# Two-batch top-3 mixture on one core: second weights issued together, bias products in pairs, product tiles stored in one transfer

## The reference, cut to what matters

```python
x_addr = x_flat @ P_w.T
dw1 = _route_dense(x_addr @ U1.T, 3, 1.0)    # 3 of 12 experts for each token, softmax weights
dw2 = _route_dense(x_addr @ U2.T, 3, 1.0)
dw3 = _route_dense(x_addr @ U3.T, 3, 1.0)
h = _apply_mixture(x_flat, dw1, W1)          # W1: 12 x 1024 x 256
h = gelu(h)
y = _apply_mixture(h, dw2, W2)               # W2: 12 x 256 x 1024
y = y + dw3 @ b2                             # b2: 12 x 256
```

## Time and profile before

| what | value |
|---|---|
| median of 3 runs | 1136.07 us (1131.33 to 1138.95) |
| the profiled execution's own time | 1138.42 us |
| its span | 1136.6 us |
| PE busy | 1054.2 us (93% of the span) |
| DVE, ACT, POOL busy | 661.0, 378.6, 285.2 us |
| DMA | 177.18 MB, mean 156 GB/s |

### The profile page before, as it was taken

The page is one execution under the profiler, slowest core; times in us unless marked ns, Lnnn a source line. Parts: engine busy times, 40 slices in busy tenths (PEclk is TensorE's granted clock), DMA queues, the critical chain, the costliest instruction groups (busy, mean ns, idle before and its releaser), DMA issues. The chain is left out here.

```text
span 1136.6 us, 20171 instructions
## 1 busy us (share of the span) xinstructions
PE 1054.2 (93%) x6560; PEld 755.9 (67%) x6560; DVE 661.0 (58%) x1532; ACT 378.6 (33%) x736; POOL 285.2 (25%) x306
## 2 busy tenths in 40 slices
PE   7999999998999999999999997899899579999996
PEld 3788854687999887788764442333367446677785
DVE  3888857765444544677686787776501245633622
ACT  0566644332112131566423332333331111122230
POOL 1221100000111001111103221166435446454441
PEclk8999999999999999999999999999999879999998
DMA  7000050000797001900024443379998958674644
GB/s 222 2 1 0 1 183 1 1 1 1 256 347 244 10 0 37 410 5 0 1 83 144 172 167 126 125 257 401 387 349 300 387 197 281 222 265 140 205 140 167
DMA packets 79833, 177.18 MB, mean 156 GB/s; under 512 B 11469, under 2 KB 31935, under 8 KB 78220
## 3 DMA queue, kind: packets, MB, share of 16 engines
q1 hardware_dynamic: 55138, 102.09, 25.0%
q0 software_dynamic: 20896, 69.75, 18.1%
q10 hardware_dynamic: 3722, 4.33, 1.2%
HBM read 126.06 MB, written 47.97 MB: 153 GB/s over the span
## 5 line engine op out<-in xcount | busy, mean ns | idle before, releaser
L2174 PE MATMUL f_psT<-W,sel 128*64 (+2 forms) x432 | 104.1, 397 | 25.5 <-DVE f_stage L2315 25.5
L2223 ACT ACTIVATE shared<-f_psH 128x512 f32<-128x512 f32 x108 | 64.5, 597 | 147.8 <-PE f_psH L2125 122.1
L2125 PE MATMUL f_psH<-W,f_xTk 128*128 (+2 forms) x216 | 101.6, 611 | 9.6 <-DVE f_stage L2298 5.4
L2438 DVE COPY shared<-f_psT 128x256 f32<-128x256 f32 x54 | 22.8, 421 | 147.1 <-PE f_psT L2174 124.8
L2125 PE MATMUL f_psH<-W,ctxT 128*128 (+2 forms) x216 | 100.9, 611 | 3.7 <-DVE f_stage L2298 2.2
L2174 PEld LDWEIGHTS f_psT<-W,sel 128*64 128x64 f32 (+2 forms) x432 | 64.9, 155 | 53.8 <-issue 34.2
L2174 PE MATMUL f_psT<-W,f_xg 128*128 (+1 forms) x432 | 97.8, 379 | 0.0
L1902 POOL DMA_INDIRECT f_xg<-xn_d,f_toks x54 | 56.9, 1054 | 140.4 <-PE f_psT L2105 111.3
L2174 PEld LDWEIGHTS f_psT<-W,f_xg 128*128 128x128 f32 (+1 forms) x432 | 79.2, 188 | 10.6 <-issue 0.2
L1902 POOL DMA_INDIRECT f_temps<-h_d,f_toks x54 | 55.5, 1027 | 92.6 <-PE f_psH L2153 61.4
L2125 PEld LDWEIGHTS f_psH<-W,f_xTk 128*128 128x128 f32 (+2 forms) x216 | 32.4, 163 | 59.6 <-issue 59.5
(11 more groups left out here) (338 smaller groups left out, 2239.3 us busy)
## 6 DMA issues: line engine op xcount, KB each, us to landing
p_d<-shared SPq DMA_DIRECT2D x108, 256.0 KB, 2.1
W<-in_f_W1T SPq DMA_DIRECT2D x12, 1024.0 KB, 17.2
W<-in_f_W2T SPq DMA_DIRECT2D x12, 1024.0 KB, 7.9
m_wg<-in_m_Wg SPq DMA_DIRECT2D x16, 512.0 KB, 3.8
m_wu<-in_m_Wu SPq DMA_DIRECT2D x16, 512.0 KB, 5.2
m_wd<-in_m_Wd SPq DMA_DIRECT2D x16, 512.0 KB, 6.1
h_d<-a_W SPq DMA_DIRECT2D x16, 512.0 KB, 7.0
f_g<-p_d SPq DMA_DIRECT2D x8, 384.0 KB, 5.2
```

The source lines that it names most:

```text
L2125: mm = pe.matmul(psH[at, n % 2, c, :], xTk[n % 2][:, k, at], weights, start=k == 0, stop=k == KD - 1)
L2174: mm = pe.matmul(psT[at, n % 2, 0:D], hT[n % 2][:, k, at], weights, start=k == 0, stop=k == KH - 1)
L2223: act.activation(po[:, n % 2, c * HH:(c + 1) * HH], psH[:, n % 2, c, :], ACT.Copy).then_inc(po_ready, 1)
L2438: dve.tensor_copy(y_out[:, n % OUTS, :], psT[:, n % 2, 0:D]).then_inc(yo_ready, 1)
```

## The change

1. The second weights: loads 2 to 11 are issued one behind the other without a wait, each load with a semaphore of its own. SP then waits for them in order and counts them up in `w2_ld`, by which PE and DVE wait; the stores of sums 8 and on come behind that on SP.
2. The bias products are done in pairs: two behind each of tiles 2 to 9 in place of one behind each of tiles 2 to 17. PE waits before a pair for the additions of the pair before. DVE adds a pair one tile later, now ahead of that tile's eviction.
3. Each product tile is stored by one transfer of 128 rows of 4 KB, issued when both halves are copied. ACT's copies of both halves wait for the whole store of tile n-2.

```diff
-                    po_stored = [[sem(f"f_po_stored{i}{c}") for c in range(2)] for i in range(2)]
+                    po_stored = [sem(f"f_po_stored{i}") for i in range(2)]
...
+                    w2_landed = [sem(f"f_w2_landed{e}") for e in range(E1)]
...
-                                wait(pe, b_done, i - 1)
+                                wait(pe, b_done, i - i % 2)
...
-                                pe.wait_ge(w2_ld, e * 16 + 16)
+                                pe.wait_ge(w2_ld, e + 1)
...
-                                if 0 <= n - BIAS_AT < TT:
-                                    bias(n - BIAS_AT)
+                                if 0 <= n - BIAS_AT < TT // 2:
+                                    for i in range(2):
+                                        bias(2 * (n - BIAS_AT) + i)
...
-                                    wait(act, po_stored[n % 2][c], 16 * (n // 2))
+                                    wait(act, po_stored[n % 2], 16 * (n // 2))
...
-                                dve.wait_ge(w2_ld, 16 * E1)
+                                dve.wait_ge(w2_ld, E1)
...
+                                if 0 <= n - BIAS_AT - 1 < TT // 2:
+                                    for i in range(2):
+                                        bias(2 * (n - BIAS_AT - 1) + i)
                                 evicted(n)
-                                if 0 <= n - BIAS_AT - 1 < TT:
-                                    bias(n - BIAS_AT - 1)
...
-                                for c in range(2):
-                                    sp.wait_ge(po_ready, 2 * n + c + 1)
-                                    sp.dma_start(p1_d[b][i][:, c * HH:(c + 1) * HH], po[:, n % 2, c * HH:(c + 1) * HH]
-                                                 ).then_inc(po_stored[n % 2][c], 16)
+                                sp.wait_ge(po_ready, 2 * n + 2)
+                                sp.dma_start(p1_d[b][i], po[:, n % 2, :]).then_inc(po_stored[n % 2], 16)
 
                             def load_w2(e):
-                                wait(sp, w2_ld, 16 * e)
-                                sp.dma_start(W2[:, e], t["f_W2T"][e]).then_inc(w2_ld, 16)
+                                sp.dma_start(W2[:, e], t["f_W2T"][e]).then_inc(w2_landed[e], 16)
...
                             sp.wait_ge(h_mm, 2 * LT)
-                            for e in range(2, E1 - 2):
+                            for e in range(2, E1):
                                 load_w2(e)
+                            for e in range(E1):
+                                sp.wait_ge(w2_landed[e], 16)
+                                sp.sem_inc(w2_ld, 1)
                             for u in range(NT, TT):
                                 store_sum(u)
-                                if u - NT < 2:
-                                    load_w2(E1 - 2 + u - NT)
```

More of the change, by code:

```diff
@@ L2041, in all_products @@
                                 for s in range(2):
-                                    for c in range(2):
-                                        pool.wait_ge(po_stored[s][c], landed(F_LAST[b] + 1, s, 2))
+                                    pool.wait_ge(po_stored[s], landed(F_LAST[b] + 1, s, 2))
                             def three(u, k):
@@ L2434, in evicted @@
                                     for s in range(2):
-                                        for c in range(2):
-                                            dve.wait_ge(po_stored[s][c], landed(LT, s, 2))
+                                        dve.wait_ge(po_stored[s], landed(LT, s, 2))
                                 wait(dve, yo_stored[n % OUTS], 16 * (n // OUTS))
```

## The result

The changed kernel takes 1122.16 us (median of 4 executions, 1119.88 to 1124.61) where the kernel before, run on the same chip, takes 1136.49 (4 executions): a ratio of 0.988, 95% interval 0.984 to 0.9921. It is 14.3 us faster. The forecast was 1111.0 in a range of 1104 to 1124: the sign and the range hold, the gain is little more than half of the 25 us that were worked out. The profiled execution took 1121.68 us, span 1119.9 (before 1138.42 and 1136.6), so the difference of the two profiles, 16.7 us, stands a little above that of the medians.

What follows compares the result with a forecast made beforehand. It took PE's 20.4 us stall for the second weights' loads as the cause to remove. Terms -21.2 - 2.3 - 2.8 + 0.5, plus 1.0, gave 1138.4 - 24.8 = 1113.6 profiled, 1111 as median; range 1104 to 1124.

Steps and rivals of the forecast that it cites:

- aside on the 358: Second weight loads: at some 358 GB/s the last would land at 896, the stage starting about a microsecond later.
- T: Time at which the last second weight lands, from bytes of queues 0 and 1 at 405 GB/s: 887.
- the first rival: Ten queued weight loads take turns from the gathers; PE waits 5 to 10 us: 1116 to 1121, chance 0.17.
- so this costs nothing: SP's stores of sums held until all weights land (887): first due about 885, buffer reused two sums on, no cost.
- the sum: Whole profiled execution: -21.2 - 2.3 - 2.8 + 0.5, then 1.0 added, giving 1113.6 us; 1111 as the median.
- the 1.0 us for late gathers: Added because gathers for sum 9 and tile 12 would land later next to a full weight stream.
- the gap at tile 12: PE's 20.4 us stall for second weights goes: start at 896.3 instead of 917.50, gain 21.2 us plus 2.3 of clock.
- no new wait: Bias pairs: DVE adds while it waits for PE anyway and products are one tile old, so no wait is added.
- the beat by bytes alone: Product stores from 764 to 806: two tiles in 8.4 us, set by bytes, so whole-tile stores cost only +0.5 us.
- Contention as the limit: Second rival: loads land as slowly as today except for the engines' idle share; time 1127.8, chance 0.12.
- Gather starvation: Queued weight loads make gathers of hidden rows and sums late between 845 and 900: 1116 to 1121, chance 0.17.
- The slow store: Third rival: a whole tile's landing doubles to 14 us, five beats cost 7 us each: +35, 1146, chance 0.05.

Runs made afterwards that it cites:

- halves_again: Changed kernel with weight 0 passed on before loads 2 to 11, weight 1 behind loads 2 and 3, products stored in halves: 1110.89 us, ratio 0.9812 to before.
- first set: Four follow-up kernels (early relay with whole tiles, the same with halves, part 1 alone, part 2 alone) on one chip, where the kernel before takes 1150.28 us.
- third set: Four early-relay kernels (halves, whole tiles, halves with single biases, halves with three loads in flight) on one chip, where the kernel before takes 1132.44 us.
- pairs_only: The kernel before with part 2 (bias products in pairs) alone: 1151.01 us, ratio 1.0012 to the kernel before.
- loads_only: The kernel before with part 1 (ten loads issued together, relay behind them) alone: 1140.15 us, ratio 0.991 to the kernel before.
- relay_early: Changed kernel with weight 0 passed on before loads 2 to 11 and weight 1 behind loads 2 and 3, whole tiles: 1135.58 us, ratio 0.9854 to before.
- after_again: The changed kernel, unchanged, run again on the second set of experiments' chip: 1144.41 us, ratio 0.9957 to the kernel before.
- after: The changed kernel itself, all three parts, in its first measurement against the kernel before: 1122.16 us, ratio 0.988.

## Why the prediction was right and wrong

The time lies in the range, but in its upper end, outside the 1104 to 1116 that the prediction called its own forecast. The range was that wide for rivals that did not come true, and it caught a loss that nobody had named: that is luck.

**Part 1, the landing (right).** Foretold: the last weight lands at 887 at 405 GB/s, between 880 and 892; it had landed by 878.9, a little ahead of that, with 422 GB/s from 844 to 870. The engines gave more than the first weights' 410. It is also more than the some 358 GB/s that the Trainium skill (HBM Reference) gives as a core's share of memory bandwidth; the same section has a core that streams alone at some 425, and with one core at work the trace agrees with that. The prediction's aside on the 358 was miscounted: with its own terms T is 909 and not 896, and the stage would start some 14 us later, not one (an estimate, as that figure is the page's). The stage's start did not wait for the loads. The Trainium skill (DMA: Bandwidth & Descriptors, "Queues, rings and completion order") has each engine take turns between the queues with work, and the first rival rested on that. The trace agrees in part: hidden rows issued from 834 to 870 landed in 10.4 us (before 7.1). It did not reach PE. The changed kernel is no full test, since PE stood while the loads were issued, and its gathers asked for less (3.86 MB from 834 to 870, before 5.82). The kernels with an early relay are: the last weight landed between 878 and 885 there too. There PE waited for no gathered rows between 845 and 900. In five of the seven that have pairs it waited once for DVE at a pair, 0.55 to 1.96 us (1.70 in `halves_again`), and at tile 12 again for staged weights, up to 2.1 us on the first set's chip.

**Part 1, the way of a landed weight to PE (the step that failed).** The prediction wrote of SP, "so this costs nothing", with an eye to the stores of sums alone, and of its issues, "If SP's issue of the ten loads blocks for long, the last landing moves with it". It looked at what a blocked issue does to the loads behind it, and not at what else stands behind it on SP: the relay of weights 0 and 1, of which weight 0 is what PE needs at 836. Measured: 10.78 us of issue (from 835.57), 10.3 us of idle PE, and 1.8 us of low clock behind it. That is 12.1 against the 8.1 us by which the span (1119.9) missed the sum's (1113.6 less the 1.8 between time and span, 1111.8). Three of the four microseconds between come back in small terms that went better than forecast: the 1.54 us that PE waited for hidden rows before, now lies inside the gap; the 1.0 us for late gathers was not needed; and from tile 12's copy to tile 53's DVE took 191.0 us (910.9 to 1101.9) against 194.7 before, 3.7 where the working had 3.2. The last one is not traced.

The medians miss by more, 11.2 us, because a second term failed: the sum took its profile to lie 2.35 us above the median, as the one before had, and this one lay 0.5 below. And the relay is not all that separates the change from its forecast. With the relay early and whole tiles the gain over the kernel before is 14.7, 14.6 and 16.9 us on three chips, where 24.8 were worked out. With halves as well it is 16.5 on the first set's chip and 21.6 on the third's. Part 3 thus holds 2 to 5 of the missing microseconds; what is left, some 4 us on the third chip and 9 on the first set's, no run explains.

**Part 1, the gap at tile 12 (right).** The idle of 20.4 us and its low clock are gone. PE goes from the turned rows at 906.05 into tile 12 at 907.17, at granted clock 1.00, as foretold; only all of it is 10.9 us later than the 896.3 worked out.

**Part 2 (right in size, wrong in its sureness).** Foretold 2.8 us, second product at 0.05; measured 2.8 in the third set (intervals overlap), second product 0.01 at most. Alone, in the kernel before, the same edit is worth nothing (1.0012, 0.9988 to 1.0035), though there tile 12 waits for the loads and only the tiles behind it count. By DVE's copies `pairs_only` took 207.6 us from tile 12 to 53 and `loads_only`, with single biases, 208.9: on that slower chip 1.3 us are left of the 3.5, which that interval can't tell from nothing. Why it is less there is not settled. And "no new wait" was wrong where the relay is early: PE waited 1.70 us for the additions in `halves_again` and 1.96 in `relay_early`.

**Part 3 (mis-sized).** Foretold +0.5 in -2 to +5; measured +2.4 alone and 1.8 and 4.7 beside the rest. The bound held, the choice of value did not. I had set the beat by bytes alone, and the beat held nearly (8.7 us against 8.4); but behind it, from 806 to 834, the engines are not kept full with whole tiles (0.89 against 0.99), and the end of the stage, where PE waits for hidden rows, is no place where a lateness is forgiven.

**The rivals.** Contention as the limit (1127.8) is out by the landing. Gather starvation is out in its size, there in waits of at most some 3 us. The slow store is out at +35 and there at 2 to 5. None named what happened. The time fell where the first rival had put it (1116 to 1122), by another mechanism.

**What stays open.** The chips of the first two sets take 14 us more for the kernel before than that of the result. Rows of PE there look alike, tile by tile; but PE's waits for staged weights from 900 to 1000 add up to 18.9 us in `after_again`, with the same kernel that has 6.7 on the first chip, and DVE and ACT are released late at certain tiles with no releaser that the trace can name. I made no run to find out why. The relay costs PE 5 to 10 us of waiting on both kinds of chip; how much of the whole gain is left differs, and that is not explained.

## What to carry to other kernels

A queue that issues transfers and also passes on semaphores is one queue: when waits are taken away from it, list everything that stands behind the issues, and put what is already due ahead of them. A burst of large loads is issued quickly only for its first few (seven here); keep a few in flight (three here, at the same rate), and the queue stays free. Passing on a landed weight early costs something too: whoever waits for one that has not landed holds the loads behind it. And a stall removed is worth what is late next, so the first question to a burst is not when its last transfer lands but who asks for its first.

## What the runs showed of the hardware that was not expected

- The issue of a load of 1 MB takes 0.43 to 0.65 us for the first seven in a row and 1.4 to 3.2 us from the eighth on (`after`, `loads_only` and `after_again` alike, though in the last the eighth takes 0.78); with three in flight, 0.33 to 0.47 us throughout. The long issues follow one another nearly as fast as such loads can land beside the gathers: 1.05 MB at 422 GB/s is 2.5 us (an estimate), the ninth and tenth take 2.7 to 3.2.
- Loads and gathers together moved 420 to 422 GB/s over 24 to 26 us on one core, with a DMA share of 1.01 to 1.02, above the 410 of the first weights.
- Two products on 32 rows each, in different row groups and banks, began within 0.01 us of each other and ended together: a tile with two takes 5.11 us, with one 5.10.
- A wait of PE of about 3 us had two outcomes: behind 3.11 us the next sixteen products took 3.71 us at granted clock 1.00, behind 2.74 us they took 5.77 at 0.62, part of it at the 1.2 GHz level.
- The same kernel took 1122.16 us on one chip and 1144.41 on another.
